# A convolution block and a selective-scan block: one GpSimd step and the first layer's image ends placed elsewhere in their orders

## The reference

```python
# layer 0, per image
h = depthwise_conv7x7(x) + conv_b
h = (h - mean_c(h)) * rsqrt(var_c(h) + 1e-5) * ln_g + ln_b     # over the 96 channels
h = gelu(h @ w1 + b1) @ w2 + b2                                 # 96 -> 384 -> 96
x = h * layer_scale + x
# layer 1
a = silu(instance_norm(x) * gamma + beta)                       # over the 3136 pixels of an image
t = windows of 8 x 8 of a                                       # 1568 windows of 64 steps
xz = layer_norm(t) @ in_proj_w;  xc, z = split(xz)              # 192 channels each
xc = silu(depthwise_conv3x3(xc) + conv_b)
# four directions k, 192 channels, 16 states
delta = softplus(dt_w @ x_dbl[:6] + dt_b)
h = h * exp(delta * A) + delta * xc * B;   y = sum_n h * C      # 64 steps, one after the other
y = layer_norm(sum of the four directions + D * xc) * silu(z)
out = x + alpha * (t + y @ out_proj_w)
```

## Time and profile before

| what | value |
|---|---|
| runs | 30521.6 us median of 3 (30518.36 to 30525.9) |
| profiled execution | 30517.93 us, its span 30516.3 us |
| granted TensorE clock | 0.993 of full speed |
| busy: PE, DVE, ACT, POOL | 93%, 91%, 80%, 82% |
| layer 0 | about 0 to 3430 us |
| layer 1 | the rest, 196 tiles |
| DMA | 3040 MB, mean 100 GB/s |

### The profile page before, as it was taken

The page is one execution under the profiler, slowest core; times in us unless marked ns, Lnnn a source line. Parts: engine busy times, 40 slices in busy tenths (PEclk is TensorE's granted clock), DMA queues, the critical chain, the costliest instruction groups (busy, mean ns, idle before and its releaser), DMA issues.

```text
span 30516.3 us, 998779 instructions
## 1 busy us (share of the span) xinstructions
PE 28431.6 (93%) x406126; PEld 12082.4 (40%) x406126; DVE 27713.6 (91%) x18447; ACT 24382.4 (80%) x39002; POOL 24950.7 (82%) x7411
## 2 busy tenths in 40 slices
PE   8999799999999999999999999999999999999998
PEld 2333344444444444444444444444444444444443
DVE  7888699999999999999999999999999999999998
ACT  4555688888888888888888888888888888888887
POOL 0000499999999999999999999999999999999998
PEclk9999899999999999999999999999999999999999
DMA  3333355555555555555555555555555555555554
GB/s 83 89 78 89 74 101 103 102 102 101 102 103 102 104 99 105 101 104 102 104 100 103 102 102 101 102 102 102 104 101 103 101 104 100 105 101 105 100 104 92
DMA packets 4881900, 3040.12 MB, mean 100 GB/s; under 512 B 3395312, under 2 KB 4198256, under 8 KB 4856880
## 3 DMA queue, kind: packets, MB, share of 16 engines
q1 hardware_dynamic: 4869824, 2905.98, 47.9%
q0 software_dynamic: 8560, 77.41, 0.7%
HBM read 2325.71 MB, written 444.78 MB: 91 GB/s over the span
## 4 chain that ended last, share of the span: by engine, by line
PE 54%; ACT 13%; DVE 9%; issue 8%; DMA 3%; SPq 1%; POOL 1%; DVEq 0%; ACTq 0%; POOLq 0%
PE dbu L1043 21%; PE pp L1138 10%; PE yb L1062 9%; DVE state L1497 6%; ACT state L1269 4%; DVE dg L1487 2%; PE pp L1131 2%; DMA xa<-act_d 2%; PE pp L1111 2%; PE pp L1119 1%; PE pp L1100 1%; PE pp L1167 1%; PE pp L1145 1%; PE pp L1120 1%; DMA dlx<-dd 1%
## 5 line engine op out<-in xcount | busy, mean ns | idle before, releaser
L1497 DVE TENSOR_TENSOR_SCAN state<-state,dbu 128x1024 f32<-128x1024 f32 x9408 | 21089.3, 2273 | 1840.9 <-PE dbu L1043 1783.3
L961 POOL TENSOR_TENSOR state<-state,cc 128x2048 f32<-128x2048 f32 x4704 | 21344.5, 4565 | 244.7 <-DVE state L1497 125.1
L1269 ACT ACTIVATE state<-dl,a_neg 128x512 f32<-128x512 f32 x18816 | 12325.3, 712 | 17.5 <-PE yb L1062 5.5
L1043 PE MATMUL dbu<-dg,du_t 64*32 64x256 f32 x301056 | 10234.8, 382 | 640.6 <-DVE state L1497 377.7
L1043 PEld LDWEIGHTS dbu<-dg,du_t 64*32 64x32 f32 x301056 | 4858.1, 106 | 6709.2 <-issue 5570.6
L1062 PE MATMUL yb<-state,mask 128*32 128x512 f32 x37632 | 5036.3, 607 | 5.8 <-POOL state L961 4.6
L1487 DVE TENSOR_TENSOR dg<-b_t,mask_q 128x1024 f32<-128x1024 f32 x3136 | 3759.5, 1199 | 53.3 <-PE b_t L1079 53.3
L969 POOL TENSOR_TENSOR dd<-sp_r,sp_w 128x512 f32<-128x512 f32 x1176 | 1506.9, 1281 | 1846.5 <-ACT sp_w L1357 1845.7
L229 POOL DMA_DIRECT2D act_d<-acted x32 | 16.3, 509 | 3210.6 <-DVE mixed L489 2904.5
L1357 ACT ACTIVATE sp_w<-pp 128x256 f32<-128x256 f32 x2352 | 903.7, 384 | 2046.3 <-PE pp L1138 2043.2
L1138 PE MATMUL pp<-sp_a,minus 128*128 128x256 f32 x4704 | 1649.7, 432 | 466.1 <-ACT ye L1297 263.3
(11 more groups left out here) (176 smaller groups left out, 27576.9 us busy)
## 6 DMA issues: line engine op xcount, KB each, us to landing
dl<-dlx SPq DMA_DIRECT2D x4704, 256.0 KB, 4.6
cc<-cd SPq DMA_DIRECT2D x3136, 256.0 KB, 5.5
dlx<-dd SPq DMA_DIRECT2D x1176, 252.0 KB, 3.2
shifted<-in_x SPq DMA_DIRECT2D x384, 392.0 KB, 12.5
xs<-ye SPq DMA_DIRECT2D x1176, 112.0 KB, 6.1
xs<-ye SPq DMA_DIRECT2D x588, 128.0 KB, 6.0
image<-in_x SPq DMA_DIRECT2D x32, 1176.0 KB, 24.5
act_d<-acted POOLq DMA_DIRECT2D x32, 1176.0 KB, 9.3
```

Of the source, the lines that this page charges most:

```text
L961: nc.gpsimd.tensor_tensor(its, its, cc[:, h, :, :].rearrange("p s x -> p (s x)"), ALU.mult).then_inc(hc_done, 1)
L1043: last = nc.tensor.matmul(dst[:, :, TQ * e:TQ * e + TQ], du_t[its, j, col:col + JC], dg[its, h, 2 * k + s, MG * TQ * g:MG * TQ * g + MG * ...
L1269: nc.scalar.activation(state[:, slot, :, m * WPX:m * WPX + WPX].rearrange("p (q k) t -> p q k t", k=2), by_place(dl[:, J // 2, 2 * h + J % ...
L1497: nc.vector.tensor_tensor_scan(its, its, dbu[p % 2][:], 0.0, ALU.mult, ALU.add).then_inc(scan_done, 1)
```

## The change

In layer 0 `finish` is cut up. On ScalarE the small part stays behind steps 0 and 7 and the Silu goes behind steps 1 and 8. On VectorE the one-column operations go to the start of steps 1 and 8, and the last product is made in three pieces of 19, 19 and 18 rows, behind steps 2, 3, 4 and 9, 10, 11; the store waits for the third. VectorE's 16 turns are all written out. In layer 1 `L_U` goes from 4 to 6, so each `step_size` and `times_u` comes two steps later in GpSimd's order, and `PP`, `DUT`, the `S_` constants and `BUILD` are changed together. ScalarE's `S_AFFINE` is the scaling of y (1398), `S_Z` the gate's projection (1126), `S_CONV` the 3x3 convolution (1111).

```diff
--- before.py
+++ after.py
@@ -16,6 +16,7 @@
 RT = ROWS * W
 NR = H // ROWS
 STEPS = 2 * NR
+THIRDS = [0, 19, 38, 56]
 HID = 4 * C
 HC3 = HID // 128
 TAPS = 7
@@ -231,7 +232,7 @@
 
                 with pool.Fori(0, NB // 2, 1) as i:
                     for par in range(2):
-                        pool.wait_ge(based, i * 2 + par + 1)
+                        pool.wait_ge(based, i * 6 + par * 3 + 3)
                         store(i * 2 + par, par)
                 for par in range(2):
                     pool.wait_ge(stored[par], NB // 2 * 32)
@@ -348,12 +349,15 @@
                     nc.scalar.activation(mlp[:], out_p[:, 0:RT], ACT.Identity, scale=vec[:, 4:5],
                                          bias=lsb[:, 0:1]).then_inc(mlp_done, 1)
 
-                def finish(i, par):
+                def deviation_of_image(i, par):
                     b = i * 2 + par
                     act.wait_ge(mv_done, b + 1)
                     nc.scalar.activation(istd[:, 0:1], mv[:, 1:2], ACT.Ln, bias=eps[:, 0:1]).then_inc(ivar_done, 1)
                     act.wait_ge(ivar_done, b + 1)
                     nc.scalar.activation(istd[:, 1:2], istd[:, 0:1], ACT.Exp, scale=-0.5).then_inc(istd_done, 1)
+
+                def silu_of_image(i, par):
+                    b = i * 2 + par
                     act.wait_ge(scale_done, b + 1)
                     nc.scalar.activation(acted[:, par, :], mixed[:, par, :], ACT.Silu, scale=scale[:, par, 0:1],
                                          bias=scale[:, par, 1:2]).then_inc(acted_done, 1)
@@ -370,9 +374,13 @@
                         leave_mlp(n)
 
                         if s == 0 and not first:
-                            finish(i - 1, 1)
+                            deviation_of_image(i - 1, 1)
+                        if s == 1 and not first:
+                            silu_of_image(i - 1, 1)
                         if s == NR:
-                            finish(i, 0)
+                            deviation_of_image(i, 0)
+                        if s == NR + 1:
+                            silu_of_image(i, 0)
 
                 squares(0)
                 deviation(0)
@@ -381,7 +389,8 @@
                     with act.Fori(1, NB // 2 - 1, 1) as i:
                         body(i)
                 body(NB // 2 - 1, last=True)
-                finish(NB // 2 - 1, 1)
+                deviation_of_image(NB // 2 - 1, 1)
+                silu_of_image(NB // 2 - 1, 1)
 
             @block.vector
             def _(dve):
@@ -475,7 +484,7 @@
                         nc.vector.tensor_copy(scale[:, par, 0:1], vec[:, 5:6])
                         nc.vector.bn_aggr(mv[:], stats[:]).then_inc(mv_done, 1)
 
-                def finish(i, par):
+                def scale_of_image(i, par):
                     b = i * 2 + par
                     dve.wait_ge(istd_done, b + 1)
                     nc.vector.tensor_tensor(scale[:, par, 0:1], scale[:, par, 0:1], istd[:, 1:2],
@@ -485,8 +494,11 @@
                     nc.vector.scalar_tensor_tensor(scale[:, par, 1:2], mv[:, 0:1], scale[:, par, 0:1], vec[:, 6:7],
                                                    ALU.mult,
                                                    ALU.subtract, reverse1=True).then_inc(scale_done, 1)
-                    dve.wait_ge(acted_done, b + 1)
-                    nc.vector.scalar_tensor_tensor(mixed[:, par, :], acted[:, par, :], vec[:, 7:8], mixed[:, par, :],
+
+                def base_of_image(i, par, part):
+                    its = slice(THIRDS[part] * W, THIRDS[part + 1] * W)
+                    dve.wait_ge(acted_done, i * 2 + par + 1)
+                    nc.vector.scalar_tensor_tensor(mixed[:, par, its], acted[:, par, its], vec[:, 7:8], mixed[:, par, its],
                                                    ALU.mult, ALU.add).then_inc(based, 1)
 
                 every = range(len(dtaps))
@@ -495,6 +507,10 @@
                     for s in range(STEPS):
                         more = s + 2 < STEPS or not last
                         ahead = (i, s + 2) if s + 2 < STEPS else (i + 1, s + 2 - STEPS)
+                        if s == 1 and not first:
+                            scale_of_image(i - 1, 1)
+                        if s == NR + 1:
+                            scale_of_image(i, 0)
                         if more:
                             conv_below(*ahead, every[:CUT])
                         if not (last and s == STEPS - 1):
@@ -506,22 +522,21 @@
                         add_image(i, s // NR, s % NR)
                         if more:
                             add_below(*ahead)
-                        if s == 0 and not first:
-                            finish(i - 1, 1)
-                        if s == NR:
-                            finish(i, 0)
+                        if 2 <= s < 5 and not first:
+                            base_of_image(i - 1, 1, s - 2)
+                        if NR + 2 <= s < NR + 5:
+                            base_of_image(i, 0, s - NR - 2)
 
                 conv_below(0, 0, every)
                 add_below(0, 0)
                 conv_below(0, 1, every)
                 normalise(0)
                 add_below(0, 1)
-                body(0, first=True)
-                if NB // 2 > 2:
-                    with dve.Fori(1, NB // 2 - 1, 1) as i:
-                        body(i)
-                body(NB // 2 - 1, last=True)
-                finish(NB // 2 - 1, 1)
+                for i in range(NB // 2):
+                    body(i, first=i == 0, last=i == NB // 2 - 1)
+                scale_of_image(NB // 2 - 1, 1)
+                for part in range(3):
+                    base_of_image(NB // 2 - 1, 1, part)
 
 
 ROW_ONE, ROW_B, ROW_C = RK, 16, 32
@@ -529,27 +544,27 @@
 N_CONSTS = 37 + 128 // TQ
 PARTS = [(2 * JB, 0), (JB, 2 * JB)]
 
-PP = [("d01", 0), ("m02", 0), ("cen", 1), ("n02", 0), ("var", 1), ("s10", 0), ("xin0", 1), ("d02", 0),
-      ("m10", 0), ("n10", 0), ("s11", 0), ("xin1", 1), ("d10", 0), ("m11", 0), ("n11", 0), ("s12", 0),
-      ("yf1", -1), ("d11", 0), ("m12", 0), ("cv0", 1), ("n12", 0), ("cv1", 1), ("ymean", -1), ("d12", 0),
+PP = [("d01", 0), ("m02", 0), ("cen", 1), ("n02", 0), ("var", 1), ("s10", 0), ("d02", 0), ("xin0", 1),
+      ("m10", 0), ("n10", 0), ("s11", 0), ("xin1", 1), ("m11", 0), ("d10", 0), ("n11", 0), ("s12", 0),
+      ("yf1", -1), ("d11", 0), ("m12", 0), ("n12", 0), ("cv0", 1), ("cv1", 1), ("ymean", -1), ("d12", 0),
       ("yvar", -1), ("xd0", 1), ("s00", 1), ("xd1", 1), ("m00", 1), ("n00", 1), ("yout", -1), ("s01", 1),
-      ("d00", 1), ("z0", 1), ("m01", 1), ("z1", 1), ("n01", 1), ("s02", 1), ("yf0", 0)]
+      ("z0", 1), ("d00", 1), ("m01", 1), ("z1", 1), ("n01", 1), ("s02", 1), ("yf0", 0)]
 
 S_CEN, S_VAR, S_NORM = 2, 4, 6
 S_YF, S_YMEAN, S_TAKEN, S_YSQ, S_YVAR, S_SCALED, S_AFFINE, S_GATED, S_YOUT, S_OUT = (
-    {19: (-1, 1), 47: (0, 0)}, 26, 28, 28, 30, 32, [32, 32], 35, 39, 41)
-S_XIN, S_CONV, S_SILU, S_XD, S_Z = [7, 13], [22, 25], 26, [32, 34], [43, 44]
+    {19: (-1, 1), 47: (0, 0)}, 27, 28, 28, 30, 32, [34, 34], 35, 39, 41)
+S_XIN, S_CONV, S_SILU, S_XD, S_Z = [8, 13], [24, 26], 27, [32, 34], [41, 44]
 
 CHAINS = [(6, 1, 0), (12, 1, 1), (18, 1, 2), (33, 0, 0), (40, 0, 1), (46, 0, 2)]
-DUT = {0: (0, 0, 1), 8: (0, 0, 2), 14: (0, 1, 0), 20: (0, 1, 1), 28: (0, 1, 2), 42: (1, 0, 0)}
-L_LOG, L_SUMS, L_U = 1, (3, 5), 4
+DUT = {0: (0, 0, 1), 7: (0, 0, 2), 16: (0, 1, 0), 20: (0, 1, 1), 28: (0, 1, 2), 42: (1, 0, 0)}
+L_LOG, L_SUMS, L_U = 1, (3, 5), 6
 SUM_COLS = TOK // 2
 S_ZSILU = 38
-S_BT = {6: 1, 41: 0}
-
-BUILD = {20: (0, 0), 21: (0, 2), 22: (0, 1), 23: (0, 3), 25: (1, 0), 26: (1, 2), 27: (1, 1), 28: (1, 3)}
-
-S_YE = [11, 15, 20, 21, 27, 30]
+S_BT = {6: 1, 35: 0}
+
+BUILD = {19: (0, 0), 20: (0, 2), 22: (0, 1), 23: (0, 3), 24: (1, 0), 26: (1, 2), 27: (1, 1), 28: (1, 3)}
+
+S_YE = [11, 13, 19, 22, 29, 31]
 AHEAD, LAG = 4, 6
 TURNS = 8
```

## The result

The changed kernel takes 31,403.1 us (median, 31,401.5 to 31,420.3) where the kernel before takes 30,521.6: 1.029 times the time, 95% interval 1.027 to 1.031. The direction was forecast, the size was not, and the time lies above the range. The profiled execution has a span of 31,399.8 us. Layer 0 is shorter (the first scan of layer 1 starts 129 us sooner) and a tile of layer 1 went from 137.94 to 143.16 us, mean of the tiles between the third and the 195th. (A tile is counted from one scan of p = 1 to the next.)

A forecast was written before the change was run, and what follows sets the result against it. No single engine bounds layer 1, a chain of waits through POOL's sum and xa does; PE bounds layer 0. 30,518 + 370 (172 ordinary tiles) - 41 (24 turning tiles) - 150 (layer 0) = 30,697, about 30,700 us; 8-in-10 range 30,230 to 31,020.

The forecast's parts named there:

- Layer 0: Layer 0 gains about 150 us: 102 from image ends and 49 from writing out DVE's turns.
- The written-out code: DVE's turns in layer 0: PE's wait of 3.28 us at each of 15 turns goes, 49 us gained.
- Rival (4): Layer 0 brings nothing because DVE's written-out code is fetched no faster than the loop's: 30,850 us, chance 0.05.
- The sum that releases xa: Layer 1, POOL's `step_size` of f = 0, j = 1: it ends 2.05 us later against the scans, and xa with it.
- The queue that the other sum is moved past: SyncE, end of a tile: dlx follows `cc`'s issue by 1.9 us, not 4.2; landing 0.9 us later, bounds 0 and 1.9.
- Rival (3): Slower by more: dlx waits for all of `cc`, ACT takes half the moves' gain; 4.35 us a tile, 31,100 us, chance 0.12.
- The decays: ACT, layer 1: they need the f = 0, j = 0 transfers about when these land, four steps in hand; no cost.
- PE's wait and the clock: Layer 1's centring matmul: PE waits about 4 us in every tile, and the lower clock behind it costs 1.3 us.
- The moves: Layer 1's moved uses give back 0.5 us a tile around the 3x3 convolution and 1.2 us by two other moves.
- (b) and (c): Layer 1: y's scaling leaves between `xd0` and `s00`, `z0` goes from 43 to 41; together 1.2 us a tile gained.
- The product at p = 20: Layer 1: it comes within 1 us of its use at p = 20, where DVE is the bound; no cost summed.
- The tiles in which PE's loop turns: 24 tiles of layer 1 where PE is late anyway: only what the moves give counts, -41 us.

The follow-up runs named there:

- theory A of that run: Layer 0 as changed but VectorE's inner 14 turns a hardware loop again, layer 1 as before: 30,425.5 us; this theory expected 30,430 us.
- the sums back: The changed kernel with L_U at 4 again, so GpSimd's sums and `times_u` go back two steps, all other moves kept: 30,291.9 us, ratio 0.992.
- only j = 0 back: The changed kernel with only the sum of f = 0, j = 0 back at its chain's first step plus 4: 30,705.3 us, ratio 1.006.
- xa is never late: Kernels with the load of xa issued ahead of the transfers of f = 0, j = 1; on the changed kernel, sums still late: 30,493.5 us.
- the fastest kernel (30,086 us): The changed kernel with all sums at plus 4 again and xa's load issued ahead of the transfers of f = 0, j = 1: 30,086.3 us, ratio 0.985.
- the one with the convolution as before: The 30,086 us kernel with the 3x3 convolution's uses, Silu and `ymean` back at their old steps, products still moved: 30,182.8 us, ratio 0.988.

## Why the prediction was wrong

**Layer 0: right.** 150 us were forecast. The runs give 150, the traces 129 to 137. The image end keeps 0.76 us, forecast 0.8, and the pieces of DVE cost nothing. The written-out code is worth 44 us by the runs and 37 by the traces' first scans, forecast 49 (theory A of that run). Rival (4) is out.

**The sum that releases xa: its lateness right, its weight wrong.** It ends 8.16 us after the start of the scan of p = 45 and not 6.09: 2.07 us, forecast 2.05. What it costs by itself no run says: with only this sum back nothing is gained, but there it ends only 0.46 us sooner and SyncE is busy with `cc` until 8.02. A price shows only with `cc` out of the way: 139.52 against 137.64, 1.9 us a tile, together with the other four sums. 1.6 of it stand in steps 1 to 9 (24.89 and 23.31), behind the later xa, and 0.3 in steps 17 to 32.

**The queue that the other sum is moved past: the first step that failed.** The forecast was that dlx follows 1.9 us after `cc` has been issued and costs 0.9 us of landing, "nearer to the median". Both numbers were wrong.

First the distance. The 1.9 doesn't come out of the prediction's own rows. The end of `cc`'s issue was put at 29.3 of the scale, and dlx at 31.1, which is where the sum of j = 1 starts (24.21 + 6.87) and not where it ends. In the kernel before, dlx is issued at 30.32:

```profile
15030.32 0.54 SPq L838 DMA_DIRECT2D dlx<-dd  x1
```

2.05 us later it is at 32.4, 3.1 us behind `cc`. The run of the sums alone (4 to 6 in the kernel before) has 2.15, near to the 1.9 by luck: dlx is where these rows put it (8.20 us after the scan of p = 45), but `cc` is out 1.0 us later than forecast (6.05 and not 5.1 after that scan). In the changed kernel the distance is 0.41 us. The other moves take the difference: they shorten the time from the scan of p = 41 to that of p = 45 by 1.5 us (12.62 to 11.12), so the sum of f = 0, j = 0, which hangs on GpSimd's pace, ends that much later against the scan of p = 45 (by 1.6 us already with the sums back, -14.9 to -13.2). I worked out each part against the scans of before and never put the moves' own gain into the distances of the queue.

Second the price. The landing took 2.8 us more (3.29 to 6.06), and xa 0.5 more (5.7 to 6.2). The bound of 1.9 was drawn from the distance, so it fell with it. The landing moves with the end of `cc` and not with its own issue, and without `cc` ahead it is 3.25 us again. The rule of the Trainium skill ("DMA: Bandwidth & Descriptors", section "Queues, rings and completion order") that a completion is posted only after earlier writes of the same DMA engine is not contradicted by the tables above, but it isn't what they show at work: the packets of dlx themselves are late, and no row has a completion held back behind them. Rival (3) had this mechanism and its point of decision (dlx less than 3 us after `cc`: it is 2.90 in the median, counted from the start of the issue of `cc`), with a chance of 0.12 and 31,100 us; the chance was too low and the price too small.

**The decays: dismissed in half a sentence, and the larger failure.** "The decays need the transfers of f=0,j=0 about when they land, with four steps in hand before the scan." The decays indeed have steps in hand, but ACT takes its work in order: while it waits 2.9 us for `dl`, the copy `zi` stands behind it, and with it PE's use of the bank, 1.75 us. From the scan of p = 45 to the next of p = 1 a tile takes 14.44 us in the changed kernel and 12.47 with only j = 0 back, where ACT's wait for `dl` falls from 546.4 to 3.9 us in all and PE's for `zi` from 342.5 to 2.5; the steps 1 to 9 behind the late xa take 26.57 and 24.89. These 1.97 and 1.68 us are the 3.6 us that the place of the sum j = 0 costs. The stretch is as long when xa is never late (15.02 against 12.50 with the sums back as well), so the 1.97 are a cost of their own beside the queue's: 386 us in 196 tiles, of the 703 between forecast and result. Here too the moves take part. With the sums alone, where the sum of j = 0 ends 10.35 us ahead of the scan of p = 45 and not 8.31, the same stretch takes 12.55 us, 0.3 more than before.

**PE's wait and the clock: right, the wait in part by luck.** Forecast a wait of about 4 us and PEclk below 1 behind it; it is 3.80 us. But L1107 begins 5.6 us later after the scan of p = 45 than it did (17.6 to 23.2) and not 2.95. The wait is no longer than forecast because the decays make PE itself come 2 us later; the two errors hide each other in this number. As to the clock, layer 1 has 1,610 us at half clock by the trace's clock records where it had 168. That is 7.4 us at half clock a tile more, though only part of it is on PE's path. The Trainium skill ("TensorE: Matmul & The Clock Gate", part 1) has the low rate as the default that activity lifts, and the trace agrees in the earlier trace rows and in the 0.62 above.

**The moves: too much.** -1.7 a tile were taken, the runs give -0.3 with xa behind the sum and -1.3 when xa is never late. Of the three waits of PE that they were to end, those behind L1297 and L1340 are gone; the one for `zi` has grown (168.9 to 342.5 us in all) because of the decays; with the sums back it is gone also (2.8 us). The part that was costed at nothing (products `dg`) is the largest, the one costed at 1.2, (b) and (c), is a part of the 0.26 left. The gain from p = 41 to 45 was there, but it went into a longer wait for xa, whose time is set by POOL and SyncE. `ymean` right behind `cv1` costs DVE a wait of 1.5 us a tile at L1521 that wasn't in the sum.

**The product at p = 20: small.** "Within 1 us of its use" turned into a wait of 1.5 us a tile on PE (L1160, 287.4 us in all). With only the two sums of this place compared (j = 0 back against all sums back), steps 17 to 32 differ by 0.3 us, since another wait of 0.5 us goes.

**The tiles in which PE's loop turns: as forecast in kind.** They didn't pay for the late xa: a mean of 139.89 us, 0.4 less than before (140.27), where 1.7 less was forecast; PE waits 0.11 us at L1107 in them.

Put together, in us a tile: moves -0.3, the sums other than j = 0 +1.9, the sum j = 0 +3.6, in all +5.2. Against the forecast for an ordinary tile (+2.15, measured +6.02) 2.15 us are missing at the end of the tile, nearly all for the decays, 0.8 in steps 1 to 9, for the late xa, and 0.9 that the moves didn't give. 196 tiles of +5.22 us less 129 make 894 us, and the spans differ by 884.

## What to carry to other kernels

When a step is moved later in an in-order queue, work out the distance to what stands ahead of it after the whole change, the gains of the other moves included; a gain just ahead of a queue bound by another engine turns into a wait. Look for the small transfer that is issued right behind a large one: its landing is then counted from the end of the large one. And where a consumer has steps in hand, ask what stands behind it on its engine, since the wait is passed on to that.

A chain that goes through an engine doesn't price it. POOL makes up 27% of the changed kernel's chain and waits 4.5 us a tile for `cc` (891.9 us in all, nearly all of it at p = 30 and 31, for the loads of the second phase); with only j = 0 back it still does,

```profile
L976 POOL TENSOR_TENSOR state<-state,cc 128x2048 f32<-128x2048 f32 x4704 | 21380.8, 4565 | 2029.6 <-DVE state L1513 1134.1 <-DMA cc<-cd 890.8
```

and the tile is 3.6 us shorter. So these waits aren't what that sum's place costs; what they cost themselves was not measured. Only an undone part gives a price.

## What the runs showed of the hardware that was not expected

Four loads of 256 KB issued ahead on the same queue delay a store of 252 KB behind them by what is left of their own transfer. Its first packet goes out 1.2 us after its issue when they are away or nearly done, and 2.7 to 3.3 us after it when the store is issued 0.1 to 0.4 us behind them; it lands in 3.3 us, and in 6.1 to 6.4. The same four loads take longer when they are issued in one go with xa and four more: 11.4 us from the start of the issue to the landing and not 8.0.

In the fastest kernel (30,086 us) PE never waits at L1107 and layer 1 still has 489 us at half clock, where the one with the convolution as before has 153; no run here tells why.
